# Third layer's attention: the order of one turn, narrower scores, keys rotated first, values in two buffers

## What is computed

```python
qkv = einsum('bsh,oh->bso', hidden_states, Wqkv)      # 32 query, 8 key, 8 value heads of 128
xq, xk = _apply_rope(xq, cos, sin), _apply_rope(xk, cos, sin)
xk, xv = repeat(xk, 4, axis=2), repeat(xv, 4, axis=2)
scores = einsum('bqhd,bkhd->bhqk', xq, xk) * scale
scores = where(causal, scores, -1e30)
out = einsum('bhqk,bkhd->bqhd', softmax(scores, -1), xv)
attn_output = einsum('bsd,hd->bsh', out, Wo)
```

## Time and profile before

| | |
|---|---|
| median of 3 runs | 1597.06 us (1591.18 to 1598.67) |
| the profiled execution | 1588.73 us, span on the core 1586.9 us |
| granted TensorE clock, mean | 0.976 |
| PE matmul busy, whole span | 1430.3 us, 90% |
| DVE, ACT, POOL busy | 1120.2, 735.7, 432.0 us |
| the attention that is changed | from 691.6 to 1408.9 us |

### The profile page before, as it was taken

How to read it: one execution, slowest core, us unless ns; L and a number is a source line. 1 busy time by engine, 2 the same in 40 slices (tenths; PEclk the granted TensorE clock), 3 DMA queues, 4 the chain that set the end, 5 groups by cost and what they waited for, 6 DMA issues and landing times.

```text
span 1586.9 us, 26588 instructions
## 1 busy us (share of the span) xinstructions
PE 1430.3 (90%) x9332; PEld 1215.0 (77%) x9332; DVE 1120.2 (71%) x2171; ACT 735.7 (46%) x1996; POOL 432.0 (27%) x328
## 2 busy tenths in 40 slices
PE   4888888869999797899999999999999999958998
PEld 3776767547777585788888988889888988846887
DVE  6686868678999853546776778767687767863554
ACT  3675757532222221425555555555555555532332
POOL 5100000003223370433343241434243342315000
PEclk9999999999999999699999999999999999988999
DMA  6000010113322000210202010020202120010000
GB/s 198 28 1 28 1 57 10 40 41 102 118 79 73 7 14 2 74 34 28 67 28 67 26 33 33 26 66 26 66 26 66 26 66 14 13 47 20 15 13 26
DMA packets 39681, 67.80 MB, mean 43 GB/s; under 512 B 4940, under 2 KB 13799, under 8 KB 39618
## 3 DMA queue, kind: packets, MB, share of 16 engines
q1 hardware_dynamic: 37522, 65.69, 13.2%
q10 hardware_dynamic: 2096, 1.30, 0.3%
HBM read 60.65 MB, written 2.13 MB: 40 GB/s over the span
## 4 chain that ended last, share of the span: by engine, by line
PE 59%; DVE 21%; issue 13%; POOL 3%; ACT 3%; DMA 1%; SPq 0%; POOLq 0%; DVEq 0%; ACTq 0%
PE PS L325 14%; PE PS L327 14%; PE PS L326 14%; DVE E_p L1253 3%; DVE A_mx L1024 2%; DVE E_nb L1244 2%; DVE E_mx L1240 2%; PE PS L1793 2%; DVE A_pT L1011 2%; DVE E_T L1262 1%; PE PS L1776 1%; PE PS L1459 1%; PE PS L1491 1%; POOL E_sw L526 1%; PE PS L1480 1%
## 5 line engine op out<-in xcount | busy, mean ns | idle before, releaser
L325 PE MATMUL PS<-XNH,E_WL 128*128 128x256 f32 x768 | 218.1, 284 | 6.7 <-POOL E_WL L440 5.9
L326 PE MATMUL PS<-XNL,E_WH 128*128 128x256 f32 x768 | 214.4, 279 | 0.0
L327 PE MATMUL PS<-XNH,E_WH 128*128 128x256 f32 x768 | 214.2, 279 | 0.0
L526 POOL TENSOR_TENSOR E_sw<-E_sw,rope2s 128x1024 f32<-128x1024 f32 x64 | 103.3, 1615 | 309.9 <-ACT E_sw L578 309.9
L1240 DVE TENSOR_REDUCE E_mx<-PS 128x4 f32<-128x512 f32 x64 | 60.8, 951 | 139.2 <-PE PS L1779 139.2
L325 PEld LDWEIGHTS PS<-XNH,E_WL 128*128 128x128 f32 x768 | 144.7, 188 | 11.1 <-POOL E_WL L440 8.9
L326 PEld LDWEIGHTS PS<-XNL,E_WH 128*128 128x128 f32 x768 | 144.5, 188 | 1.0
L327 PEld LDWEIGHTS PS<-XNH,E_WH 128*128 128x128 f32 x768 | 144.4, 188 | 0.0
L791 ACT ACTIVATE E_p<-PS,E_nb 128x128 f32<-128x128 f32 (+1 forms) x256 | 103.8, 431 | 85.1 <-DVE E_nb L1244 85.1
L578 ACT ACTIVATE E_sw<-PS 64x256 f32<-64x256 f32 (+1 forms) x128 | 89.5, 699 | 103.8 <-PE PS L327 102.3
L440 POOL TENSOR_TENSOR E_WL<-raw,E_WH 128x512 fp32r<-128x512 f32 x80 | 102.7, 1319 | 124.6 <-ACT E_WH L578 124.6
(11 more groups left out here) (266 smaller groups left out, 4260.3 us busy)
## 6 DMA issues: line engine op xcount, KB each, us to landing
raw<-in_w SPq DMA_DIRECT2D x104, 256.0 KB, 2.9
words<-in_words SPq DMA_DIRECT2D x11, 768.0 KB, 4.3
wo<-in_wo SPq DMA_DIRECT2D x32, 256.0 KB, 3.9
zb<-z_scratch SPq DMA_DIRECT2D x11, 384.0 KB, 5.1
scb<-in_scales SPq DMA_DIRECT2D x11, 384.0 KB, 5.6
X<-in_x SPq DMA_DIRECT2D x8, 256.0 KB, 5.7
SGH<-XNH SPq DMA_DIRECT2D x8, 256.0 KB, 2.7
SGL<-XNL SPq DMA_DIRECT2D x8, 256.0 KB, 2.9
```

The source lines that it names most:

```text
L325: nc.tensor.matmul(o, sl, mh, start=first, stop=False)
L326: nc.tensor.matmul(o, sh, ml, start=False, stop=False)
L327: return nc.tensor.matmul(o, sh, mh, start=False, stop=last)
L526: nc.gpsimd.tensor_tensor(E_sw[:, heads, :], E_sw[:, heads, :], rope2s[:, :].unsqueeze(1).broadcast_to([P, heads.stop - heads.start, SEQ]) ...
```

## The change

- PE's turn is now: scores of i-1; key and value projection; the four query projections; transposes of the probabilities; transposes of the values; both halves of the output projection; weighted values, now into banks 0 and 1. Bank 2 still takes keys and values.
- The scores of the first 128 queries cover only the first 128 keys. Each mask matmul covers two heads (2x128 columns) and comes after all four heads of its block, so there are 4 instead of 8.
- The keys are rotated before the queries on ACT, POOL and DVE, and finished (`QKH`, `QKL`) before the queries start.
- The values' H and L parts have two buffers each.
- On ACT `next_heads` (j = 3) and the rounding for the fourth layer (j = 2) now stand after the rounding of the queries and before the rounding of the weighted values (`OH`). The weight tiles of a group are stored keys and values first.
- PE's waits go with it: the scores wait for the queries' rest (`qlo`) and for both residual additions of the turn before (`x`), as they did, but now they open the turn.

```diff
-                VH = sb(st, "VH", [P, 2, P], F32R)
-                VL = sb(st, "VL", [P, 2, P], F32R)
+                VH = [sb(st, f"VH{p}", [P, 2, P], F32R) for p in range(2)]
+                VL = [sb(st, f"VL{p}", [P, 2, P], F32R) for p in range(2)]
...
             def l2_sines(i, n):
-                heads = (slice(0, 4), slice(4, 5))[n]
+                heads = (slice(4, 5), slice(0, 4))[n]
...
                 if step:
                     act.wait_ge(e2["pk"], i + 1)
+                    after(act, e2["q"], i * 2)
                     copy(E_sw[0:64, 4, :], PS[64:P, 2, 0:SEQ])
                     copy(E_sw[64:P, 4, :], PS[0:64, 2, 0:SEQ], e2["sw"])
                     after(act, e2["vtp"], i)
                     copy(vT2[:, :], PS[:, 2, SEQ:2 * SEQ], e2["vt"])
+                    act.wait_ge(e2["q"], i * 2 + 1)
+                    after(act, e2["sc"], i * 2)
+                    copy(QKH[:, 4, :], E_T[:, 4, :], e2["qhi"])
+                    act.wait_ge(e2["pq"], i + 1)
+                    qs = PS[:, 0:2, :].rearrange("p n (h t) -> p (n h) t", h=2)
+                    copy(E_sw[0:64, 0:4, :], qs[64:P, :, :])
+                    copy(E_sw[64:P, 0:4, :], qs[0:64, :, :], e2["sw"])
...
+                    act.wait_ge(e2["q"], i * 2 + 2)
+                    copy(QKH[:, 0:4, :], E_T[:, 0:4, :], e2["qhi"])
+                if more_heads is not None:
+                    more_heads()
                 if one:
                     for tb in range(2):
                         act.wait_ge(e2["pv"], i * 2 + (tb - 1))
...
-                        copy(OH[q][:, tb, :], PS[:, 3 + tb, :], e2["ohi"])
-                if more_heads is not None:
-                    more_heads()
+                        copy(OH[q][:, tb, :], PS[:, tb, :], e2["ohi"])
...
                 if step:
                     cosines(*K)
+                    rotated(*K)
+                    rotated_rests(*K)
+                    cosines(*Q)
+                if one:
+                    probability_rests(0, slice(0, 1))
+                if step:
                     rotated(*Q)
                 if one:
...
+                    probability_rests(1, slice(1, 3))
                 if two:
                     add_branch(0)
                 if step:
-                    rotated(*K)
+                    dve.wait_ge(e2["vhi"], i + 1)
+                    V.tensor_tensor(VL[j % 2][:, :, :], PS[:, 2, SEQ:2 * SEQ].rearrange("p (s d) -> p s d", s=2), f32(VH[j % 2][:, :, :]),
+                                    ALU.subtract).then_inc(e2["vlo"], 1)
                     rotated_rests(*Q)
-                    rotated_rests(*K)
                 if two:
                     add_branch(1)
...
                     for tb in range(2):
-                        t = slice(tb * P, (tb + 1) * P)
+                        t, keys = slice(tb * P, (tb + 1) * P), slice(0, (tb + 1) * P)
                         for h in range(4):
                             at, bank = (h % 2) * SEQ, 3 + 2 * tb + h // 2
...
+                            o = PS[:, bank, at:at + (tb + 1) * P]
+                            mm(o, QKL[:, h, t], QKH[:, 4, keys], start=(h % 2 == 0), stop=False, skip_group_check=True)
+                            mm(o, QKH[:, h, t], QKL[:, 4, keys], start=False, stop=False, skip_group_check=True)
+                            mm(o, QKH[:, h, t], QKH[:, 4, keys], start=False, stop=False, skip_group_check=True)
+                        for e in range(2):
+                            seen = PS[:, 3 + 2 * tb + e, :].rearrange("p (h s) -> p h s", h=2)[:, :, tb * P:(tb + 1) * P]
+                            last = mm(seen, identb[:, :], mask_ts[:, :].unsqueeze(1).broadcast_to([P, 2, P]), start=False, stop=True,
                                       skip_group_check=True)
                         last.then_inc(e2["sc"], 1)
                 if step:
                     after(pe, e2["vlo"], i)
-                    project(range(4, 6), e2["pk"])
-                if two:
-                    output(0)
+                    project(range(2), 2, e2["pk"])
+                    if two:
+                        pe.wait_ge(e2["olo"], i * 2 - 2)
+                    elif i == 1:
+                        pe.wait_ge(e2["t1"], 2)
+                    project(range(2, 6), 0, e2["pq"])
```

More of the change, by code:

```diff
@@ L771, in _, with l2_slot @@
             finish(act, 5)
-            def l2_slot(g, j, step, one, two, next_heads=None, more_heads=None):
+            def l2_slot(g, j, step, one, two, more_heads=None):
                 i, q = g * NB + j, 1 - j % 2
[L777 to L782, removed]
                 if one:
@@ L807, in l2_slot @@
                 if step:
[L808 to L814, removed]
-                    act.wait_ge(e2["vtp"], i + 1)
-                    after(act, e2["pv"], i * 2)
-                    copy(VH[:, :, :], PS[:, 2, SEQ:2 * SEQ].rearrange("p (s d) -> p s d", s=2), e2["vhi"])
+                    act.wait_ge(e2["vtp"], i + 1)
+                    if not isinstance(i, int) or i >= 2:
+                        act.wait_ge(e2["pv"], i * 2 - 2)
+                    copy(VH[j % 2][:, :, :], PS[:, 2, SEQ:2 * SEQ].rearrange("p (s d) -> p s d", s=2), e2["vhi"])
+                    act.wait_ge(e2["q"], i * 2 + 2)
+                    copy(QKH[:, 0:4, :], E_T[:, 0:4, :], e2["qhi"])
+                if more_heads is not None:
+                    more_heads()
                 if one:
@@ L840, in l2_group @@
                 for j in range(NB):
-                    l2_slot(g, j, True, not first or j >= 1, not first or j >= 2, next_heads if j == NB - 1 and more else None,
-                            {1: wo_heads, 2: sum_head}.get(j))
+                    l2_slot(g, j, True, not first or j >= 1, not first or j >= 2,
+                            {1: wo_heads, 2: sum_head, 3: next_heads if more else None}.get(j))
             l2_group(0, True, True)
@@ L1283, in l2_slot @@
                     maxima(1)
-                if step:
-                    cosines(*Q)
-                if one:
                     probabilities(0)
@@ L1311, in l2_slot @@
                         dve.wait_ge(e2["ohi"], i * 2 + (tb - 1))
[L1312 removed]
+                        V.tensor_tensor(OL[q][:, tb, :], PS[:, tb, :], f32(OH[q][:, tb, :]), ALU.subtract).then_inc(e2["olo"], 1)
                 if final:
@@ L1736, in l2_slot, with project @@
                 i, p = g * NB + j, j % 2
-                def project(units, signal):
-                    for u in units:
+                def project(units, bank, signal):
+                    for n, u in enumerate(units):
                         pe.wait_ge(w_lo, g * U_L2_G + (U_L2 + u + 1))
@@ L1742, in project @@
                             span, tok = slice(k * P, (k + 1) * P), slice(j * SEQ, (j + 1) * SEQ)
-                            last = product3(PS[:, u // 2, (u % 2) * SEQ:(u % 2 + 1) * SEQ], E_WH[:, u, span], E_WL[:, u, span],
+                            last = product3(PS[:, bank + n // 2, (n % 2) * SEQ:(n % 2 + 1) * SEQ], E_WH[:, u, span], E_WL[:, u, span],
                                             XNH[:, k, tok], XNL[:, k, tok], k == 0, k == KT - 1)
@@ L1752, in output @@
                             pe.wait_ge(e2["x"], i * 2 - 4)
+                        if not one:
+                            pe.wait_ge(e2["plo"], i * 2 - 2)
                         if j == 2:
@@ L1759, in output @@
                     last.then_inc(e2["wo"], 1)
-                if step:
-                    if not isinstance(i, int) or i >= 1:
-                        pe.wait_ge(e2["t1"], i * 2 - 1)
-                    project(range(4), e2["pq"])
                 if one:
@@ L1795, in l2_slot @@
                         last.then_inc(e2["pt"], 1)
-                if two:
-                    output(1)
                 if step:
                     pe.wait_ge(e2["vt"], i + 1)
-                    pe.wait_ge(e2["t1"], i * 2 + 2)
+                    pe.wait_ge(e2["t1"], i * 2 + 1)
                     for s in range(2):
@@ L1803, in l2_slot @@
                     last.then_inc(e2["vtp"], 1)
+                if two:
+                    output(0)
+                    output(1)
                 if one:
                     pe.wait_ge(e2["vlo"], i)
+                    if step:
+                        pe.wait_ge(e2["t1"], i * 2 + 2)
                     for tb in range(2):
```

33 lines of the change are left out of this document (12 added, 21 removed).

## The result

The changed kernel takes 1638.5 us (median), the kernel before 1594.6 on the same chip: ratio 1.028, 95% interval 1.025 to 1.031. That is 44 us slower, where 13 were forecast, and lies outside the range. The profiled execution's span is 1637.0 us against 1586.9, at a mean clock of 0.952 against 0.976.

What follows compares the result with a forecast made beforehand. PE was taken to bound every turn before; afterwards the queries' rotation chain would add a wait. Start +0.5, turns +9.2, end +2.1 and clock +1.5 gave +13 us: median 1597.06 + 13 = 1610 us, range 1589 to 1625.

Steps and rivals of the forecast that it cites:

- start, first projection to first score: Ahead of the first scores: now 16.4 us; 8.42 of projections plus a chain of 8.46 afterwards, so +0.5 us.
- first to last turn's scores: From first to last score: 678.95 us now, 688.1 after, +9.2, with groups of four turns at 89.05 against 88.26.
- end: After the last scores: first output half (2.8 us) no longer covers the last softmax, less 0.7 from scores: +2.1.
- clock: At the start, PE idles 8.2 us; 1.5 us added for one more stretch at mostly 1.2 GHz.
- the scores: PE's score matmuls and masks in a turn: 3.84 us falls by 0.68 to 3.16.
- the gone wait for weights: PE's 0.85 us wait for weights, once in a group, goes because they are needed later than before.
- turns j = 2: POOL's sums delay DVE's addition by 1.2 us and the queries' rest by 0.3: turn of 23.0 us.
- j = 3: POOL's first weight rest starts 0.3 us ahead of the queries' rest and costs 1.0 (0 to 1.3): turn of 22.5.
- the plain turn: Turn j = 1: scores 3.16, projections 8.42, chain 9.95, so 21.53 us, 0.26 less than now.
- the race at j = 1: POOL's rests start 0.15 us behind the queries' rest, cost 0; rival, race lost: 1.2 in 8 groups, 1620 us, 15%.
- PE bounds every turn: Kernel before: PE busy 695.8 of 717.3 us, idle only 0.2 in a turn and 0.85 once in a group.
- lay off the path: DVE's negation of the maxima, 2.04 us where POOL's large product runs: its stall goes, but was not on the path.

## Why the prediction was wrong

The direction was right, the size was not. Of the 50.1 us between the spans, 4.5 arose ahead of the attention, in code that did not change (its first projection starts at 696.18, at 691.63 before). They are a difference of the two executions: 58.0 us at half the clock lie ahead of it against 44.4, and the kernels of all runs here, of either order, start it between 691.5 and 698.6. The rest by the steps of the sum:

| term | forecast | measured |
|---|---|---|
| start, first projection to first score | +0.5 | 16.91 - 16.34 = +0.6 |
| first to last turn's scores | +9.2 | 718.6 - 679.0 = +39.6 |
| end | +2.1 | 205.3 - 200.0 = +5.4 |
| clock | +1.5 | in the rows above |

**Right:** the scores (3.16; 3.20 measured), the matmul over 128 columns (0.11), the gone wait for weights, the 8 us idle at the start (8.02), turns j = 2 (23.0; 23.04 measured, with 1.0 on the addition and 0.4 on the queries' rest where 1.2 and 0.3 were forecast) and j = 3 (22.5; 22.50), and the plain turn, once POOL is out of the way (21.53; 21.63). DVE's queue sets the turn, and its long instructions are those that meet one of POOL's.

**Wrong, the clock.** This is the step that failed, as a term of the sum that was far too small: "I add 1.5 for one more such stretch", at the start. In turns 2 to 31 the slow stretches cost 20.9 us (each turn's time above that of the same j at the full clock: eleven of about 1.56, one of 3.13, and 0.64 in turn 2), and turn 1, with 10.1 us at half the clock, took 23.8 instead of 20.25. Together 24.4 of the 30.4 us by which the middle row was missed, against the 1.5. That the 3.5 of turn 1 are all the clock's is argued and not shown, since no run of the new order has this turn at the full clock. The sum had short idle times in every turn and priced each at its length. The earlier trace rows showed the half clock behind PE's first waits, but I took it for something of the start. The run with six extra matmuls shows the cost directly: the median fell by 22 us when PE had more to do, 19.3 of it between the first and the last turn's scores in the traces.

**Wrong, the race at j = 1.** A margin of 0.15 was priced at 0, and the lost race at 15%. Counted from 1095.36, which is 0.28 ahead of ACT's copies as in the forecast's chain, POOL started at 8.09 (forecast 8.2) and DVE's rest at 8.14 (8.07). Each step was right to 0.1, which is not enough for a margin of 0.15. Seven turns at +1.2 make 8.4. Turns j = 0 came out 0.4 below the forecast, 2.7 in all. With 0.3 of small pieces this closes the row: 24.4 + 8.4 - 2.7 + 0.3 = 30.4.

**Wrong, what bounded the kernel before.** "PE bounds every turn", and the negation's stall "lay off the path". PE's 0.20 us wait ahead of the transposes was that path's end: narrow scores alone gained nothing, and the negation on ACT gave 12 us at once. It did not enter the sum for this change, but it hid that a better use of the narrow scores was in the old order.

**Half right, the end.** 2.1 of 5.4. Two extra stretches at the half clock lie there (6.8 and 3.4 us). In the run with six extra matmuls, whose code behind the last scores is the same, 7.9 us less of the end lie at half the clock, and the end takes 202.5, +2.5 against before. So the forecast's mechanism covers the end but for 0.4, and the other 2.9 go with the clock.

The Trainium skill ("SBUF — State Buffer", section "SBUF: two separate sides") has DVE with two SBUF inputs and POOL take turns for whole instructions. The trace agrees: 2.33 instead of 1.22 at j = 1, and 1.21 again with POOL held back. The Trainium skill's 81 ns for a stream of matmuls over 128 columns ("TensorE: Matmul & The Clock Gate", section "Back-to-back issue gap") isn't met here: 110 ns.

## What to carry to other kernels

A wait that recurs in every turn can have two prices, its length and the clock behind it, and here the second was highest when narrow matmuls followed. Look in the trace at the clock and at what follows the wait; if the wait must stay, try wide work next to it. Before shortening the busiest engine's work, follow its smallest recurring wait back: 0.2 us per turn was a second bound that took the whole gain. And where two engines race within a tenth of a microsecond, price the lost race and hold one of them back by a semaphore.

## What was not expected of the hardware

- In these runs the half clock came by the pair of wait and work behind it, not by the idle time alone. From 760 to 1400 us: waits of 1.64 us ahead of transposes in 27 turns, no slow stretch; of 2.25 there, with narrow scores elsewhere in the turn, 6; of 1.96 ahead of wide scores, 3; of up to 1.83 ahead of wide scores, 2; of up to 1.83 ahead of narrow scores, 13; of 1.96 ahead of narrow scores, 36. Why the same wait does it in one turn and not in the next stays open; in the changed kernel all turns j = 0 had it, with 1.6 us idle ahead of their scores, and no turn j = 1, with 0.7.
- Matmuls over 128 columns run every 0.11 us, nearly as long as over 256 (0.117), but at half the clock they take 0.21, as the wide ones do.
- A negation of 128x4 on DVE, 0.17 us long when POOL is still, took 2.04 us behind POOL's product in 22 of the 31 turns before and 1.6 to 2.0 in the others. Among PE's waits it showed only as the 0.20. On ACT it takes 0.20.
